# Small-head attention: how the row maxima get into q's stack, and when they are computed

## The reference, cut to what matters

```python
def _L1_attn_ref(x, Wq, Wk, Wv, Wo):          # x: (4, 1024, 128)
    q = (x @ Wq.T).reshape(B, S, 16, 8)       # k, v alike
    q = q * cos - jnp.roll(q, 1, axis=-1) * sin   # k alike
    scores = jnp.einsum('bhqd,bhkd->bhqk', q, k) / math.sqrt(8)
    attn = jax.nn.softmax(scores, axis=-1)
    ctx = jnp.einsum('bhqk,bhkd->bhqd', attn, v)
    return ctx.reshape(B, S, 128) @ Wo.T
```

## Time and profile before

| | us |
|---|---|
| median of 3 runs | 4477.36 |
| the profiled execution | 4475.59 |
| its span, first to last instruction | 4473.8 |
| the stage's scores, first to last | 2087 to 2858 |
| busy in the whole span: TensorE | 3975.3 (89%) |
| VectorE | 3385.5 (76%) |
| ScalarE | 2913.3 (65%) |

### The profile page before, as it was taken

How to read it: one execution, slowest core, us unless ns; L and a number is a source line. 1 busy time by engine, 2 the same in 40 slices (tenths; PEclk the granted TensorE clock), 3 DMA queues, 4 the chain that set the end, 5 groups by cost and what they waited for, 6 DMA issues and landing times. The chain is left out here.

```text
span 4473.8 us, 88017 instructions
## 1 busy us (share of the span) xinstructions
PE 3975.3 (89%) x34586; PEld 2227.3 (50%) x34588; DVE 3385.5 (76%) x4741; ACT 2913.3 (65%) x4403; POOL 2240.4 (50%) x1443
## 2 busy tenths in 40 slices
PE   6999999999999979996877777899788877999999
PEld 3666667666666654442111211245677543444443
DVE  6888888888884547767898899565877657878887
ACT  3777777777776449982677777685556644555555
POOL 2888888888886013331121210172566554555555
PEclk7999999999999989996899999898899988999999
DMA  3212212212210011100121100142000224454544
GB/s 84 59 40 59 58 38 59 59 40 58 58 35 16 1 49 48 71 24 29 50 74 43 40 27 16 57 149 72 11 13 15 75 83 115 113 124 116 120 113 108
DMA packets 113913, 270.28 MB, mean 60 GB/s; under 512 B 24276, under 2 KB 36308, under 8 KB 111004
## 3 DMA queue, kind: packets, MB, share of 16 engines
q1 hardware_dynamic: 98084, 223.86, 18.7%
q0 software_dynamic: 15424, 40.89, 2.6%
HBM read 178.10 MB, written 50.81 MB: 51 GB/s over the span
## 5 line engine op out<-in xcount | busy, mean ns | idle before, releaser
L522 POOL TENSOR_TENSOR a_prob_low<-a_prob_whole,a_prob_high 128x1024 f16<-128x1024 f32 x512 | 1085.0, 2131 | 276.7 <-ACT a_prob_high L412 275.6
L496 DVE TENSOR_REDUCE a_part_max<-a_top 128x2 f32<-128x1024 f32 x512 | 626.2, 1223 | 218.7 <-PE a_top L323 212.6
L409 ACT ACTIVATE a_prob_whole<-a_score 128x1024 f32<-128x1024 f32 x512 | 525.2, 1026 | 332.5 <-PE a_score L312 320.5
L976 ACT ACTIVATE a_prob<-a_score 128x512 f32<-128x512 f32 x1024 | 533.1, 603 | 255.9 <-PE a_score L915 255.8
L1009 DVE TENSOR_REDUCE a_part_max<-a_side 128x2 f32<-128x1024 f32 x512 | 595.2, 1220 | 68.3 <-PE a_side L886 68.3
L412 ACT ACTIVATE a_prob_high<-a_score 128x1024 f16<-128x1024 f32 x512 | 521.8, 1019 | 0.0
L311 PE MATMUL a_score<-a_qa,a_ka 128*128 128x256 f16 x2048 | 476.8, 273 | 0.0
L312 PE MATMUL a_score<-a_qb,a_kb 128*128 128x256 f16 x2048 | 476.5, 273 | 0.0
L2185 POOL TENSOR_TENSOR m_lows<-m_scaled,m_high 128x512 f16<-128x512 f32 x264 | 311.2, 1183 | 323.8 <-ACT m_high L2146 322.2
L378 PE MATMUL a_o_ps<-a_v,a_prob_high 128*128 128x65 f16 x4096 | 428.2, 193 | 6.2 <-POOL a_prob_low L522 3.4
L380 PE MATMUL a_o_ps<-a_v,a_prob_high 128*128 128x64 f16 x4096 | 427.0, 194 | 0.0
(11 more groups left out here) (477 smaller groups left out, 10147.8 us busy)
## 6 DMA issues: line engine op xcount, KB each, us to landing
m_gate<-gates SPq DMA_DIRECT2D x264, 256.0 KB, 5.2
a_ka<-a_nat_high_k SPq DMA_DIRECT2D x128, 128.0 KB, 2.4
e_gate<-gates SPq DMA_DIRECT2D x8, 2048.0 KB, 7.2
slots<-in_slots SPq DMA_DIRECT2D x19, 520.0 KB, 4.2
a_qa<-a_nat_high_q SPq DMA_DIRECT2D x64, 128.0 KB, 2.4
a_qa<-a_nat_low_q SPq DMA_DIRECT2D x64, 128.0 KB, 2.4
a_qb<-a_nat_high_q SPq DMA_DIRECT2D x64, 128.0 KB, 2.4
a_kb<-a_nat_low_k SPq DMA_DIRECT2D x64, 128.0 KB, 2.4
```

Of the source, the lines that this page charges most:

```text
L409: eng.activation(prob_whole[:, e % RING, :, :, :], score[:, e % 2, :, :, :], ACT.Exp, scale=scale)
L496: eng.tensor_reduce(part_max[:, i, c, :, qt % 4], top[:, :, :], AX.X, ALU.max).then_inc(max_done, 1)
L522: eng.tensor_tensor(prob_low[:, e % RING, :, :, :], prob_whole[:, e % RING, :, :, :], prob_high[:, e % RING, :, :, :], ALU.subtract).then_ ...
L976: eng.activation(prob[:, e % RING, h, :], score[:, step % SLOTS, :], ACT.Exp).then_inc(exp_done, 1)
```

## The change

- The max jobs start 13 events ahead instead of 11 (unit 0's second half stays where it was).
- The shift of the first half moves from 2 to 4 events ahead of the unit, into event 12; that of the second half from event 6 to event 4 (unit 0's stays in event 7).
- The maxima take 16 columns (4 heads x 4 query tiles) instead of a mostly zero 128, so the turned result has 16 rows. VectorE writes them negated in fp16 to a tile `shift` (one instruction) instead of adding them to q's stack with four.
- SyncE carries the 16 rows to DRAM, waits for that, and loads them with four DMAs, one for each head, into one row of q's stack. The scores of a half wait for these four (`shift_in`) instead of for VectorE.
- SyncE's list is put in another order: the loads of units 0 and 1 come first, and the load of unit n + 1 stands between the two shifts of unit n. The store of a batch comes after the second shift of the batch's third unit.

```diff
-                    put(start - 2, "shift", n, 0)
+                    put(start - 4, "shift", n, 0)
                 for m in range(16):
-                    put(start - 11 + 8 * i + m // 2 if n or not i else m // 2, "max", n, 16 * i + m)
+                    put(start - 13 + 8 * i + m // 2 if n or not i else m // 2, "max", n, 16 * i + m)
...
-            put(start + (6 if n else 7), "shift", n, 1)
+            put(start + (4 if n else 7), "shift", n, 1)
             put(start + 12, "turn", n, 0)
             put(start + EV + 4, "turn", n, 1)
...
-        part_max = pl.sb("part_max", [P, 2, 2, HEADS, 32])
-        row_max = pl.sb("row_max", [P, 2, P])
+        part_max = pl.sb("part_max", [P, 2, 2, HEADS, 4])
+        row_max = pl.sb("row_max", [P, 2, 4 * HEADS])
+        shift = pl.sb("shift", [4 * HEADS, 2, P], F16)
...
+                def turned_shift(n, i):
+                    eng.wait_ge(side_freed, nth["shift", n, i] + 1)
+                    if n:
+                        eng.wait_ge(shift_in[i], 16 * HEADS * n)
+                    eng.dma_start(shifts[i, :, :], shift[:, i, :]).then_inc(shift_out[i], 16)
+                    eng.wait_ge(shift_out[i], 16 * (n + 1))
+                    for h in range(HEADS):
+                        row = 32 * h + 3 * DH
+                        eng.dma_start(qa[row:row + 1, n % 2, i * BANK:(i + 1) * BANK],
+                                      shifts[i, 4 * h:4 * h + 4, :].rearrange("t q -> (t q)").unsqueeze(0)).then_inc(shift_in[i], 16)
+
                 store(0)
+                load(0)
+                load(1)
                 for n in range(units):
-                    if n % GROUPS == 3 and n // GROUPS + 1 < B:
+                    turned_shift(n, 0)
+                    if 0 < n < units - 1:
+                        load(n + 1)
+                    turned_shift(n, 1)
+                    if n % GROUPS == 2 and n // GROUPS + 1 < B:
                         store(n // GROUPS + 1)
-                    load(n)
...
-                        mm = eng.transpose(side[:, 0, 0:P], row_max[:, job[2], :], ident[:, :])
+                        mm = eng.transpose(side[0:4 * HEADS, 0, 0:P], row_max[:, job[2], :], ident[:, :])
...
                     if first and k % kts == 0:
-                        eng.wait_ge(side_freed, nth["shift", n, k // kts] + 1)
+                        eng.wait_ge(shift_in[k // kts], 16 * HEADS * (n + 1))
...
-                eng.memset(part_max[:, :, :, :, :], 0.0).then_inc(filled, 1)
...
                     elif what == "shift":
-                        for qt in range(4 * job[2], 4 * job[2] + 4):
-                            here = qa[:, n % 2, qt * P:(qt + 1) * P]
-                            op = eng.scalar_tensor_tensor(out=here, in0=side[:, 0, 0:P], scalar=less[:, qt:qt + 1], in1=here,
-                                                          op0=ALU.mult, op1=ALU.add)
+                        if n:
+                            eng.wait_ge(shift_out[job[2]], 16 * n)
+                        op = eng.tensor_scalar(shift[:, job[2], :], side[0:4 * HEADS, 0, 0:P], -1.0, None, ALU.mult)
```

More of the change, by code:

```diff
@@ L712, in vector_rest, with small_attention @@
                 self.then(eng, eng.tensor_copy(self.slot_of[:, j, :], self.where[:, :]))
-def small_attention(nc, stage, res_t, xn_t, w, wo, ident, less, rope, w_moe_d, b_moe_d, split_d, split_out, route,
+def small_attention(nc, stage, res_t, xn_t, w, wo, ident, rope, w_moe_d, b_moe_d, split_d, split_out, route,
                     rows, slot_of, slots_d, cleared, cleared_count, scattered, w_e_in, b_e_in):
@@ L789, in small_attention @@
         planes = nc.dram_tensor(f"{stage}_planes", (B, 2, 4, P, N), F16, kind="Internal").ap()
+        shifts = nc.dram_tensor(f"{stage}_shifts", (2, 4 * HEADS, P), F16, kind="Internal").ap()
         side_banks = pl.ps("side", [P, 2, 2, BANK])
@@ L814, in small_attention @@
         stack_in = [pl.sem(f"stack_in{r}") for r in range(2)]
+        shift_out = [pl.sem(f"shift_out{i}") for i in range(2)]
+        shift_in = [pl.sem(f"shift_in{i}") for i in range(2)]
         side_full = pl.sem("side_full")
@@ L832, in _ @@
                 pl.clear_before(eng)
-                eng.wait_ge(filled, 3)
+                eng.wait_ge(filled, 2)
                 def store(b):
@@ L1008, in _ @@
                         qt, pair, c = job[2] // 4, job[2] // 2 % 2, job[2] % 2
-                        op = eng.tensor_reduce(part_max[:, qt // 4, c, 2 * pair:2 * pair + 2, 24 + qt], side, AX.X, ALU.max)
+                        op = eng.tensor_reduce(part_max[:, qt // 4, c, 2 * pair:2 * pair + 2, qt % 4], side, AX.X, ALU.max)
                     elif what == "shift":
-                        for qt in range(4 * job[2], 4 * job[2] + 4):
-                            here = qa[:, n % 2, qt * P:(qt + 1) * P]
-                            op = eng.scalar_tensor_tensor(out=here, in0=side[:, 0, 0:P], scalar=less[:, qt:qt + 1], in1=here,
-                                                          op0=ALU.mult, op1=ALU.add)
+                        if n:
+                            eng.wait_ge(shift_out[job[2]], 16 * n)
+                        op = eng.tensor_scalar(shift[:, job[2], :], side[0:4 * HEADS, 0, 0:P], -1.0, None, ALU.mult)
                     elif what == "turn":
@@ L3041, in program @@
                 ("avg", "bias0", "ident", "rowmask0", "w_b0", "bias_b0", "w_g0", "b_g0", "tri", "dest2", "base2", "sort1", "w_g1", "w_qkv1",
-                 "w_o1", "less1", "rope", "bias2", "w_g2", "mask2", "w_route")}
+                 "w_o1", "rope", "bias2", "w_g2", "mask2", "w_route")}
         avg_in = pl.sem("avg_in")
@@ L3077, in program @@
             with nc.sbuf_tensor("rows1", [P, 2, NT, P + 2], F32) as rows, nc.sbuf_tensor("slot_of1", [P, 2, NT], U32) as slot_of:
-                small_attention(nc, "a1", res_t, xn_t, kept["w_qkv1"], kept["w_o1"], kept["ident"], kept["less1"], kept["rope"], d["w_moe1"], d["b_moe1"], split_d, split_out,
+                small_attention(nc, "a1", res_t, xn_t, kept["w_qkv1"], kept["w_o1"], kept["ident"], kept["rope"], d["w_moe1"], d["b_moe1"], split_d, split_out,
                                 (kept["w_g1"], kept["tri"], kept["ident"], kept["dest2"], None, rows, slot_of, 1e-9, kept["sort1"], w_row),
@@ L3125, in lay_out @@
     rope[:, :, 0], rope[:, :, 1] = table / np.float32(np.sqrt(8.0)), table
-    less1 = np.where(p % 32 - 24 == j[:, 0:8], -1.0, 0.0).astype(np.float32)
     def narrow(w):
@@ L3161, in lay_out @@
         "ident": np.eye(P, dtype=np.float32), "tri": (p <= j).astype(np.float32),
-        "rowmask0": rowmask0, "less1": less1,
+        "rowmask0": rowmask0,
         "bias0": a["L0_attn_bo"].reshape(P, 1), "w_qkv0": w_qkv0,
```

## The result

The changed kernel takes 4548.29 us (median of 5 runs, 4529.28 to 4557.73), the kernel before 4477.36 beside it: 1.0158 times as long, 95% interval 1.0134 to 1.0183. That is +71 us where +17 was forecast, outside the range. The profiled execution is the fastest of the five (4529.28, a span of 4527.5: +53.7).

A forecast was written before the change was run, and what follows sets the result against it. Plain events were taken as bound by the loop TensorE, ScalarE, TensorE, with VectorE only keeping up. Unit 0's waits 9.6 + its moved maxima 3 + steady units 5.1 - tail 0.9 = +16.8: 4475.59 becomes 4492.4, median 4494; range 4474 to 4516.

The forecast's parts named there:

- Event 4: Second half's shift, behind the turn, must wait for the event's second maximum: +0.81 us; event 6 gives back 0.45.
- Event 12: First half's shift ahead of two maxima and a turn: event lasts 3.9 to 4.0; event 14 gives back 0.59, net 0.0.
- The plain unit: Units 2, 3, 6, 7, 10, 11, 13 and 14: net +0.36 us each, 2.9 for eight.
- Units 4, 8, 12: Event 6 also holds a "back"; without the shift it gives back all of event 4's 0.81: net 0.
- Units 1, 5, 9: ScalarE splits the next batch in event 5; event 6 can give back only 0.07: +0.74 each, 2.2 together.
- Unit 0: No cover for its two shifts: +4.8 us each, together 9.6; four max jobs moved into events 3 and 4: +3.
- The way by DMA: SyncE's store, wait and four loads: 5.7 us, bounds 4.6 and 9.5; hidden at events 4 and 12, not in unit 0.
- The tail: At the end, unit 15's event 4 loses two maxima and its wait: -0.9 us.
- rival 3: TensorE's clock falls to 1.2 GHz, about 8 us a fall; two more falls give 4510; chance 0.10.
- The load: First max job moves from event 5 to event 3; the next unit's load stays hidden, by only 0.7 us.
- rival 2: Cover breaks: load's last piece 1.9 us late, 14 units wait 1.2 each, or DMA way takes 9.0: 4511; chance 0.12.
- Rival 1: VectorE, busy 565 of 632 us, is the bound; less VectorE work makes the kernel faster, 4458; chance 0.10.

The follow-up runs named there:

- Experiment 6: The changed kernel with only the second half's shift moved, from event 4 to event 5: 4488.91 us, ratio 1.0041.
- Experiment 5: The kernel before with one added wait: behind event 4's turn, TensorE waits until the event's second maximum is reduced; no job moved: 4491.5 us, ratio 1.0043.
- experiment 3: The changed kernel with both shifts moved one event on, to events 13 and 5, which hold no turn: 4484.6 us, ratio 1.0025.
- experiment 7: The changed kernel with only the first half's shift moved, from event 12 to event 13: 4504.05 us, ratio 1.0074.
- Experiment 8: The changed kernel with maxima 11 events ahead again and shifts in events 13 and 5: 4468.72 us, ratio 0.9986.
- experiment 10: The kernel of experiment 9 with the second half's shift put ahead of event 5's two maxima: 4453.66 us, ratio 0.9952.
- experiment 11: The kernel before, masked additions and no DMA, with shifts in events 13 and 5 ahead of their maxima: 4475.85 us, ratio 0.9996.
- experiment 9: The kernel of experiment 8, but unit 0 keeps the masked additions instead of the way by DMA: 4456.84 us, ratio 0.9964.

## Why the prediction was wrong

**The steps were right, and their sum nearly.** In the profiled execution, measured against forecast:

- Event 4: 4.13 - 3.38 = +0.75 (+0.81). Event 6 gave back 0.44 (0.45). Event 12: +0.58 (+0.6), event 14 gave back 0.59 (0.59). The plain unit: 43.93 - 43.63 = +0.30 (+0.36), so +2.4 for eight.
- Units 4, 8, 12: unit 8, which had no fall, 48.53 against 48.70, -0.2 (0). Units 1, 5, 9: unit 5, 52.77 against 52.07, +0.7 (+0.74). Together +1.6 (2.2).
- Unit 0: the first scores 3.91 - 1.19 = +2.7 (+4.8), its event 7 9.35 - 6.76 = +2.6 (+4.8), its events 3 and 4 +4.1 (+3). The way by DMA was 3.6 from the store's issue, not 5.7: below my lower bound of 4.6, because the store landed in 1.35 and four loads were issued in 1.12, faster than the rows that the forecast went by. Event 14 gave back 0.6. (The first shift's VectorE instruction itself began 2.2 later than before, at 2088.34 instead of 2086.12; why was not looked into.) Event 12 took 9.01 instead of 5.89, but at a granted clock of 0.54 instead of 0.99: the fall that began in event 7, around the second wait for the way by DMA (2.63), lasted 31 us instead of 17. That +3.1 is clock for the most part, no step of the sum, and so are the 0.5 that event 0 gave back.
- The tail: unit 15's event 4 fell to 2.59, -0.8 (-0.9).

That sums to 2.4 + 1.6 + 2.7 + 2.6 + 4.1 - 0.6 - 0.8 = 12.0, against 16.8. Experiment 6, with the same quiet unit and nearly the clock of before, took 18 us more than the kernel before.

**The step that failed is the clock.** The sum was made with the clock left as it was, and rival 3 put "From 2206 to 2838, with TensorE busy for 505 of 632 us, the clock stayed at 2.4 GHz; that is against it", priced two falls and gave it 0.10. The mechanism was rival 3's in kind; its two falls were priced at 16 us, and the clock took more than twice that in the profiled execution and some four times that in the median run. Units 1 to 15 grew by 740.53 - 697.69 = 42.8. The steps account for 2.4 + 1.6 - 0.8 = 3.2 and the load's two waits for 2.7; 36.9 are left, and 155 - 39 = 116 us more were run at 1.2 GHz. That is 0.32 for each. It is near what an event loses: one of 2.39 lasts 3.70 at 1.2 GHz, and 1.31 / 3.70 is 0.35. In the median run of five, 582 us against some 400, the clock's part is then, as an estimate, 0.32 to 0.35 x 180 = 58 to 63 of the 71; with the 12 of the steps and 3 of the load that is a little more than was measured.

What misled me was the busy share. It is the same in both kernels, 34.80 of 43.63 before and 34.57 of 43.93 after; a share over a unit does not show whether the clock is close to falling. What changed is where the idle time lies. In event 4 there are two waits, of 0.34 and 0.47, on either side of the turn's 0.66; in units 1, 5 and 9 the wait for the split grew from 1.25 to 1.91, where the forecast had looked at event 6 only for the 0.07 that it could give back; and in units 3 and 4 the load was late. Experiment 5 shows that a wait like the first by itself sets off falls; experiments 3, 6 and 7 show that taking the shifts out of the turn events takes most of the loss away. What the wait for the split does by itself no run tested; the count above is what speaks for it, and in the profiled execution it has the largest part (75 of 119 us).

The Trainium skill (TensorE: Matmul & The Clock Gate, "HAM oscillation — how this bites in real kernels") tells of waits for a DMA of some 3 to 5 us that bring the slow clock back each time. The wait for a load in unit 3 agrees in kind, with 1.63. The waits of event 4 differ: they are for VectorE, below 0.5 each, and lead to a fall only sometimes; the wait for the split is for ScalarE. The measurement decides here.

**The load.** "Hidden, by only 0.7" was the smallest margin named, and rival 2 priced it for 14 units. It broke in two: rival 2's "queues that are empty then" was read from one unit, and in units 3 and 4 GpSimd's copies share the DMA engines. Experiment 8, with the first max job back in event 5, has no such wait and no fall there; the wait's own 2.7 us are small, the fall behind it is not.

**Rival 1** (VectorE as the bound) is excluded: VectorE's work in units 1 to 15 fell from 600.53 to 576.29 and nothing came of it: the stretch grew from 697.69 to 740.53. It had something, though, that the forecast put in no term: in an event of its own a shift saves 0.79 by the DMA form (experiments 10 and 11). The change spent that by putting the shift beside a turn.

**What stays open**: why the clock falls in event 4 of unit 13 and not in that of unit 10, with the same waits, and behind the wait for the split in units 1 and 9 and not in unit 5; and how the loss of 71 us divides between these waits, since one shift sets two of them.

## What to carry to other kernels

When jobs are moved on a list that TensorE runs in order, look at which waits of TensorE get longer or come in a row, also in events that hold no moved job, and not only at the sum of the times: here the clock cost some 60 us, five times the 12 of the moved work, in the main behind waits that grew by 0.7 us or less and a late load in two units. A busy share like that of before is no argument that the clock will hold; price several falls, from the trace's own slow stretches, wherever a change adds waits to events that repeat. And a way by DMA that is hidden in the steady state should leave the first unit alone, where nothing hides it: that was worth some 10 us (experiments 8 and 9).

## What the runs showed of the hardware

- A store of 16 rows, 4 KB, from SBUF to DRAM landed in 1.35 us, and the whole way, from the store's issue to the first scores that read the loaded rows, took 3.6.
- The VectorE instruction on 16 x 128 took 0.27 to 0.28; the masked addition on 128 x 128 took 0.344. The forecast's 0.25 stood between this and the 0.19 of the earlier trace rows.
- A fall to 1.2 GHz lasts differently long behind the same kind of wait: in the changed kernel 61 us behind the wait for the split in unit 1, 14 in unit 9 and none in unit 5; 7 and 14 us in event 4 of units 12 and 13. A kernel's runs differ by this: the five of the changed kernel have 534 to 601 us at 1.2 GHz and spans of 4527.5 to 4555.9.
- A fall needs no long wait: in the 8 us before the one in event 4 of unit 13 no wait of TensorE ahead of a matmul was longer than 0.47 us, and the event before had been run at 2.4 GHz.
- A load of 8 x 64 KB was late by 1.63 and 1.09 us where another queue moved 0.53 and 0.63 MB beside it, and in time where that was 0.13 MB.
